# Query projection ahead of the third score unit, key projection behind the sums, maxima transposed last, and two waits for GpSimd's additions

## The reference

```python
x = x + _L0_attn_ref(_layernorm(x), ...)          # softmax(g * cos(q, k)) @ v, 16 heads of 8
x = x + _L0_ffn_ref(_layernorm(x), ...)           # top-1 of 8 experts, hidden 32
x = x + _L1_attn_ref(_layernorm(x), ...)          # causal, 16 heads of 64:
#   q, k, v = x @ w_q, x @ w_k, x @ w_v
#   a = softmax(mask(q @ k.T / 8));  y = (a @ v) @ w_o
x = x + _L1_ffn_ref(_layernorm(x), ...)           # top-2 of 8 experts, hidden 512, then a layer norm
```

## Time and profile before

| | |
|---|---|
| device time, median of 3 runs | 1553.49 us (1552.97 to 1562.78) |
| profiled execution | 1558.71 us, its span 1557.0 us |
| TensorE matmul busy | 1333.0 us, 86% of the span |
| VectorE, ScalarE, GpSimd busy | 62%, 55%, 39% |
| mean granted TensorE clock | 0.94 |
| the 64 steps of the pairs | 159 to about 1309 us |

### The profile page before, as it was taken

One profiled execution on the slowest core, in us unless ns is written; L12 is line 12 of the kernel. 1 busy time (PEld: TensorE's weight loads), 2 busy tenths in 40 slices (PEclk: granted clock), 3 DMA queues, 4 the chain that ended last, 5 costly groups with the idle time before them and its releaser, 6 DMA issues.

```text
span 1557.0 us, 28423 instructions
## 1 busy us (share of the span) xinstructions
PE 1333.0 (86%) x9302; PEld 805.6 (52%) x9302; DVE 960.1 (62%) x3308; ACT 863.6 (55%) x1679; POOL 604.2 (39%) x783
## 2 busy tenths in 40 slices
PE   3777898998899889998999899979888886988982
PEld 1233445554455445544554455545555554877872
DVE  3566655666666666766666656564665563675784
ACT  3765665656565656565566565745443453554563
POOL 1000332233243424332533254325344455556675
PEclk8879999999999999999999999989999998999997
DMA  8060990000000000000000000000102001142322
GB/s 316 1 240 1 9 4 1 1 8 8 1 13 10 8 1 15 8 8 1 15 8 8 1 15 1 8 1 24 45 8 78 4 8 35 39 112 59 111 82 87
DMA packets 65454, 54.67 MB, mean 35 GB/s; under 512 B 41016, under 2 KB 51648, under 8 KB 65056
## 3 DMA queue, kind: packets, MB, share of 16 engines
q1 hardware_dynamic: 60768, 43.48, 14.3%
q0 software_dynamic: 4544, 9.38, 1.8%
HBM read 21.03 MB, written 31.81 MB: 34 GB/s over the span
## 4 chain that ended last, share of the span: by engine, by line
PE 64%; DVE 21%; ACT 8%; issue 3%; another core or an unknown queue 1%; POOL 1%; DMA 0%; SPq 0%; ACTq 0%; POOLq 0%; DVEq 0%
PE outs L1757 9%; PE scores L1739 9%; PE work L1679 9%; DVE scores L1233 6%; PE outs L1883 6%; PE work L1786 4%; PE outs L1962 4%; PE scores L1708 3%; ACT a_buf L943 3%; DVE a_buf L1202 3%; PE work L1769 3%; PE scores L1870 3%; DVE ra L1226 2%; ACT ra L949 2%; PE scores L1950 2%
## 5 line engine op out<-in xcount | busy, mean ns | idle before, releaser
L1233 DVE CUSTOM_DVE_ANT_0 scores<-scores,mask_qk 128x512 f32<-128x512 f32 (+3 forms) x512 | 239.0, 518 | 207.0 <-PE scores L1708 203.1
L937 ACT ACTIVATE big<-scores 128x1024 f32<-128x1024 f32 (+1 forms) x192 | 169.4, 882 | 264.4 <-PE scores L1739 262.1
L786 POOL TENSOR_SCALAR_AFFINE_SELECT big<-big 128x256 f32<-128x256 f32 x256 | 101.6, 409 | 550.0 <-ACT big L937 549.8
L943 ACT ACTIVATE a_buf<-scores 128x1024 f32<-128x1024 f32 x256 | 248.9, 1029 | 51.9 <-PE scores L1870 51.6
L1739 PE MATMUL scores<-ra 64*128 64x512 f32 (+3 forms) x1536 | 186.6, 348 | 30.1 <-ACT big L937 17.5
L802 POOL TENSOR_TENSOR big<-big 128x768 f32<-128x768 f32 x64 | 116.7, 1823 | 125.5 <-DVE parts L1268 86.1
L1757 PE MATMUL outs<-big 128*64 128x512 f32 (+3 forms) x1024 | 163.8, 465 | 0.0
L1739 PEld LDWEIGHTS scores<-ra 64*128 64x128 f32 x1536 | 122.8, 190 | 77.9 <-ACT big L937 34.7
L1226 DVE TENSOR_TENSOR ra<-work,ra 128x512 fp32r<-128x512 f32 x128 | 88.3, 690 | 120.9 <-ACT ra L949 120.8
L1883 PE MATMUL outs<-a_buf 128*16 128x512 f32 x1024 | 145.1, 642 | 1.5 <-ACT a_buf L943 1.4
L1018 ACT ACTIVATE big<-scores,b_sb 128x128 f32<-128x128 f32 x312 | 89.4, 369 | 77.9 <-PE scores L1950 37.6
(11 more groups left out here) (223 smaller groups left out, 2600.2 us busy)
## 6 DMA issues: line engine op xcount, KB each, us to landing
sorted_rows<-xrows SPq DMA_DIRECT2D x34, 520.0 KB, 6.8
qkT<-sorted_rows SPq DMA_DIRECT2D x78, 65.0 KB
a_buf<-in_w SPq DMA_DIRECT2D x2, 2048.0 KB, 8.0
a_buf<-in_x SPq DMA_DIRECT2D x8, 256.0 KB, 2.7
x_rows<-x SPq DMA_DIRECT2D x8, 256.0 KB, 2.0
ra<-x_rows SPq DMA_DIRECT2D x8, 256.0 KB
a_buf<-choice_rows SPq DMA_DIRECT2D x6, 256.0 KB, 3.9
yT<-choice_rows SPq DMA_DIRECT2D x5, 256.0 KB
```

The lines of the kernel that those rows point to most:

```text
L937: activation(prob1(g, i), d[:, :, 0:256] if i == 2 else d, ACT.Exp, scale=SCALE1).then_inc(unit_free("pair", g, i), 1)
L943: activation(prob0(c)[:, i * 1024:(i + 1) * 1024], unit_wait(act, "cosine", c, i), ACT.Exp).then_inc(unit_free("cosine", c, i), 1)
L1233: return v.tensor_tensor_reduce(scores_, scores_, mask_qk[:, SEQ - width:SEQ], -1.0, 3e38, ALU.add, ALU.min, neg_max[:, qt, j:j + 1])
```

## The change

In each step the query projection of pair g+2 goes ahead of score unit 2 of pair g, the key projection goes from behind the transposed maxima to behind the sums and the item that follows them, and so the maxima are transposed last. The order of the work banks follows. ScalarE waits for score unit 2 before it copies the query's high part, does that ahead of the exponential of unit 2, and inverts the sums right behind their logarithm. VectorE takes the query's low part ahead of the maxima of unit 2. GpSimd gets two more waits ahead of its additions: in step 3 for the rows of `standardize("a0", ...)`, and in step 5 for those of the third `standardize("f0", ...)`.

```diff
# work_order
+    add(o.pair(2), ("q", o.pair(2)))
     add(o.pair(-1), ("sum", o.pair(-1)))
-    add(o.pair(2), ("q", o.pair(2)))
...
+    add(o.pair(2), ("k", o.pair(2)))
     add(o.pair(1), ("mT", o.pair(1)))
-    add(o.pair(2), ("k", o.pair(2)))
# GpSimd, sum_blocks
+                if p == 3 and h is not None:
+                    pool.wait_ge(rows_ready["a0"], h + 1)
+                if p == 5 and f is not None:
+                    pool.wait_ge(rows_ready["f0"], f * 3 + 3)
                 if g:
                     work_wait(pool, "sum", g - 1)
# ScalarE
+                if o.pair(2) is not None:
+                    if o.pair(0) is not None:
+                        unit_wait(act, "pair", o.g, 2)
+                    hi_part("q", q_hi, o.pair(2))
                 if o.pair(0) is not None:
                     score_exp(o.g, 2)
...
                 if o.pair(-1) is not None:
                     inverse_sums(o.pair(-1))
-                if o.pair(2) is not None:
-                    hi_part("q", q_hi, o.pair(2))
+                    sums_inverted(o.pair(-1))
...
-                if o.pair(-1) is not None:
-                    sums_inverted(o.pair(-1))
+                if o.pair(2) is not None:
+                    hi_part("k", k_hi, o.pair(2))
                 if o.pair(1) is not None:
                     moved(neg_max_T[:, o.pair(1) % 2, :], "mT", o.pair(1))
-                if o.pair(2) is not None:
-                    hi_part("k", k_hi, o.pair(2))
# VectorE
+                if o.pair(2) is not None:
+                    lo_part("q", q_hi, q_lo, o.pair(2), 2 * o.pair(2) + 1)
                 if o.pair(1) is not None:
                     maxima(o.pair(1), 2)
                     maxima_parts(o.pair(1))
-                if o.pair(2) is not None:
-                    lo_part("q", q_hi, q_lo, o.pair(2), 2 * o.pair(2) + 1)
# TensorE
+                if o.pair(2) is not None:
+                    project("q", 0, o.pair(2))
                 if o.pair(0) is not None:
                     score_unit(o.g, 2)
                 if o.pair(1) is not None:
                     max_unit(o.pair(1), 2)
                 if o.pair(-1) is not None:
                     sums1(o.pair(-1))
-                if o.pair(2) is not None:
-                    project("q", 0, o.pair(2))
...
+                if o.pair(2) is not None:
+                    project("k", 1, o.pair(2))
                 if o.cosine(0) is not None and o.i >= 0:
                     values0(o.cosine(0))
                 if o.pair(1) is not None:
                     max_transposed(o.pair(1))
-                if o.pair(2) is not None:
-                    project("k", 1, o.pair(2))
```

More of the change, by code:

```diff
@@ L788, in causal, with sum_blocks @@
                                         channel_multiplier=-1).then_inc(prob_masked, 1)
-            def sum_blocks(g, p, s, h):
+            def sum_blocks(g, p, f, s, h):
                 causal(g, 2, 0)
@@ L851, in _ @@
                 if o.pair(0) is not None:
-                    sum_blocks(o.g, p, o.s, h)
+                    sum_blocks(o.g, p, f, o.s, h)
                 if p == 0 and f is not None:
```

## The result

The changed kernel takes 1480.84 us (median of 4 runs, 1479.71 to 1482.35) against 1553.23 for the kernel before (4 runs, 1551.82 to 1562.78). The ratio is 0.9524, with a 95% interval of 0.9490 to 0.9557. That is 72.4 us less, where 37 were forecast, and it lies outside the range.

What follows compares the result with a forecast made beforehand. TensorE, busy for 86% of the span, was taken as the bound. Passes 1 to 4 gave 27.2 us, 0 and 5 6.9, the end 4.3: 38.4 off 1553.5, forecast 1516 us, range 1500 to 1540.

Steps and rivals of the forecast that it cites:

- the order: Moved query and key projections with their copies and low parts, without GpSimd's new waits: 1.6 us gained in all.
- Step 5's wait: GpSimd's additions wait for VectorE's scaling, so operand transposes start earlier: 2.7 + 1.2 = 3.9 us in passes 0 to 5.
- the clock term: End of step 5: fewer slow matmuls behind TensorE's shorter wait, 1.2 us a pass, bounds 0.5 and 2.1.
- Step 3's wait: Seam of steps 3 and 4: TensorE's wait and slow values behind it go, 1.75 + 1.6 = 3.35 us, passes 1 to 4.
- Rival 4: L1202 in steps 3 and 5 is long for another reason than GpSimd's additions: about 1552 us, chance 0.03.
- step 0's sum: VectorE's sum of two SBUF operands at L1538 meets GpSimd's additions: 0.3 us lost, bounds 0 and 0.5.
- The query ahead: Query projection before score unit 2 fills TensorE's slot wait in steps 2, 4 and 6: 0.85 us a pass.
- The odd steps: Operand transposes wait for the key's low part: 0.5 us lost in step 1, 0.35 in step 7, nothing in step 3.
- The last passes: Passes 6 and 7, no cosine work: key projection's wait goes, 3.5 us gained, plus 0.8 in step 5 of pass 6.
- rival 1: The order gives more: all idle time ahead of units 2 goes, nothing lost behind the key; 1495 us, chance 0.12.
- rival 3: Items behind the key wait for its bank, 1.12 us in each of 60 steps: slower, 1584 us, chance 0.05.
- the direction: Whole kernel: faster, meaning below 1538 us, at 0.84; within 1% at 0.11; slower at 0.05.

Runs made afterwards that it cites:

- k_only: The kernel before with only the key projection moved ahead of the values of the cosines and the transposed maxima, no new waits; 1573.8 us, ratio 1.0137.
- q_waits_kfirst: `q_waits` with the key's low part ahead of the normalisation on VectorE; 1502.3 us, ratio 0.9626 to the kernel before.
- q_waits: The kernel before with the query projection ahead and both waits of GpSimd's additions, key and maxima left where they were; 1479.2 us, ratio 0.9461.

## Why the prediction was wrong, point by point

The sum gave the two waits 36.8 us and the order 1.6. The waits measured 37.8 and the order 38.0 by itself. So the terms of the order failed, and above all the one for the query. By passes, 1 to 4 saved 10.7 to 12.3 us each where the sum has 6.8, and passes 0 and 5 saved 7.9 and 7.2 where it has 3.45.

**Step 5's wait** was right in mechanism and near in size: 3.9 us a pass forecast, 3.4 measured in steps 5 and 6 together. The first set of transposes waits now, 1.32 us and not 1.75; the clock term, taken as 1.2 between 0.5 and 2.1, was nearer the lower end.

**Step 3's wait** was right: 3.35 us forecast, 3.54 measured in step 4. Rival 4 is refuted: L1202 is long because of GpSimd's additions. Of what they meet when they come later I had named only step 0's sum. They now meet the scaling in step 2 too, median 457 and up to 1432 ns in the kernel after, where before the median was 339 and the longest 583:

```profile
L1207 DVE TENSOR_SCALAR xrows<-x,mean,rstd x32: 333/457/1432, 346.9 to 1278.3; 128x128 f32<-128x128 f32 x32
```

Step 2 is none the longer for it.

**The query ahead** is the step that failed: "TensorE gains the slot's idle time, 0.25 to 0.3 each: 0.85 in a pass". It is 0.79 us in step 2 alone and 44.3 us in all. Three things were wrong. I took the bracket for the whole idle time, and in step 2 it shows half of it. I left out the wait between score unit 2 and maximum unit 2 altogether, though its row stands in the list of waits behind the one that I used; it goes too, 0.32 us in step 2:

```profile
PE scores L1708 <- DVE neg_max L1233: 16.2, 52, 2.5
```

And I gave the order nothing for the clock, which stays up in more of steps 3 and 6 when waits ahead of them go, some 2 us a pass by the estimate above.

**The odd steps** were to lose by the key: 0.5 in step 1, 0.35 in step 7. The losses are there, but they are the smaller part. In step 1 of the kernel after both sets wait for the key's low part and the output projection for their copy:

```profile
611.73 0.85 PE L1861 MATMUL work<-ident_r,parts 128*128 128x128 f32 x8 [0.48 <-DVE ra L1231]
...
613.02 1.16 PE L1791 MATMUL work<-wo_sb,yT 128*128 128x128 f32 x8 [0.44 <-DVE qkT L1284]
```

Step 1 is nevertheless 0.35 us shorter. From score unit 2 to maximum unit 2 it is 0.57 us there and was 0.90, so that wait goes in odd steps too. And I had priced the query at 0.9 us there "where there was no idle time". Behind another projection it costs less, because TensorE starts its matmuls 0.23 us apart and only the last one before another kind of work takes 0.33. Its timeline in the kernel after:

```profile
604.35 0.50 PE L1684 MATMUL work<-wqkv_hi,x_hi 128*128 128x512 f32 x1
...
605.15 0.40 PE L1684 MATMUL work<-x_hi,wqkv_hi 128*128 128x512 f32 x1
...
605.94 0.62 PE L1744 MATMUL scores<-ra 64*128 64x256 f32 x6
```

From the first projection to score unit 2 it is 1.59 us, for two projections, and 0.69 more than the 0.90 for one before (638.45 to 639.35).

**Step 0's sum** of two SBUF operands, priced at 0.3 us: it meets the additions in passes 0 to 6, as said, and mostly takes 0.80 instead of 0.68. The row gives least, median and most in ns:

```profile
L1543 DVE TENSOR_TENSOR res<-a_buf,attn x8: 691/799/1478, 89.3 to 1023.7; 128x512 f32<-128x512 f32 x8
```

By the Trainium skill's rule (SBUF — State Buffer, Who interferes with whom) it was to wait out the addition in progress, and the trace agrees. In pass 0 that addition had 0.93 us left when the sum began, and the sum lost 0.80; in the other six passes it had 0.23 to 0.26 left, and the sum lost 0.10 to 0.12. What the prediction had wrong is where in an addition the sum would begin: it reckoned with a rest of up to 1.3 us. The next addition pays as well, 1.60 us for 1.27. Pass 1 of the kernel after:

```profile
309.59 1.82 POOL L806 TENSOR_TENSOR big<-big 128x768 f32<-128x768 f32 x1 [1.14 <-DVE neg_max_hl L1255]
311.18 0.79 DVE L1543 TENSOR_TENSOR res<-a_buf,attn 128x512 f32<-128x512 f32 x1
311.49 1.60 POOL L809 TENSOR_TENSOR big<-big 128x512 f32<-128x512 f32 x1
```

Step 0 as a whole gained 0.9 to 1.2 us. Of these 0.7 come with the waits alone and not with either one; I have not found how, and it stays open.

**The last passes**, 6 and 7, were to gain 4.3 us with step 5 of pass 6, and took 215.2 us for 225.2, so 10.1 less. In pass 6 the granted clock rose from 0.93 to 0.96; how much of the gain that makes is not measured.

**The rivals.** The result lies beyond rival 1, which gave "the order gives more" 1495 us at a chance of 0.12, and in part for its reason: the query covers idle time in odd steps as well as in even ones. Its argument against, VectorE's chain in odd steps, was weaker than I held it. The wait that rival 3 priced is real, in `k_only`, where the query has its old place. The chances went by the direction, which was right at 0.84.

## What to carry to other kernels

Measure what an item in an engine's queue costs, or what a gap is worth, from start to start of its neighbours, and compare it with the same pair of neighbours where nothing waits; the idle time that a profile prints behind a modelled end can be half of it. Work that is to fill a wait must leave its buffer early as well, or the wait moves one item on. And an instruction that turns up at several lengths, such as the scaling at 1.1, 3.0 and 4.25 us, points to what ran beside it: making the other engine wait a microsecond or so was worth 3.4 us a time here. Last, before calling a gain of a few us a pass the removal of a wait, compare the granted clock of the steps: part of it can be a stretch that ran slow and no longer does.

## What the runs showed of the hardware

VectorE's scaling from SBUF to SBUF stood still while GpSimd added in SBUF, 4.25 us for 1.10, while VectorE's subtraction at L1226, which reads PSUM, kept its 0.69 us. Rows 3 don't show the second, since L1257 and L1226 begin there as the last addition ends; in step 3 of the same pass they do run side by side:

```profile
682.72 1.82 POOL L802 TENSOR_TENSOR big<-big 128x768 f32<-128x768 f32 x1 [3.91 <-DVE parts L1268]
683.44 0.69 DVE L1226 TENSOR_TENSOR ra<-work,ra 128x512 fp32r<-128x512 f32 x1 [0.26 <-ACT ra L949]
```

New to me was how little idle time can stand ahead of a fall of TensorE's clock. In `q_waits_kfirst` waits of 0.50 and 0.65 us, 1.2 us apart, were followed by a stretch at the lower level. The first of them is this, the other is shown above:

```profile
623.96 0.54 PE L1862 MATMUL work<-ident_r,parts 128*128 128x128 f32 x4 [0.50 <-DVE ra L1232]
```

In the same step of `q_waits` the 0.50 is there as well and the 0.65 is not, and the output projection runs at its full speed:

```profile
608.79 0.53 PE L1862 MATMUL work<-ident_r,parts 128*128 128x128 f32 x4 [0.50 <-DVE ra L1232]
609.38 3.84 PE L1792 MATMUL work<-wo_sb,yT 128*128 128x128 f32 x32
```

That step of `q_waits_kfirst` also had the wait of 0.72 us some 13 us earlier, so the 0.65 isn't the only difference. Its granted clock was 0.93 as a whole, and 0.50 behind the two waits:

```profile
607.27:630.55 23.28, 21.04 (x148) 14.05 (x149) 15.43 (x63) 12.81 (x24) 8.02 (x10) 0.93 0.05 12
...
626.00:628.00 2.00, 2.00 (x12) 0.50 0.00 0
```

Nor do the same waits always have the same effect. In the changed kernel step 5 ends with waits of about 1.33 and 0.54 us in each of passes 0 to 4, in all three profiled executions; step 6 behind them took 17.4 us in four of these fifteen cases and 18.4 to 19.0 in eleven.
